# Own scores and row maxima as 128x128 tiles, the own weight spread through memory, value products in two runs a group

## The chip, the cores and the metric

One core of one Trainium2 chip runs the whole kernel. The metric is device time in microseconds, the median of a few executions. TensorE does the matrix products; VectorE, ScalarE and GpSimd do elementwise work; SyncE issues most transfers, and ScalarE issues some too.

## The reference

Eight batch rows of 512 tokens and 512 features pass two layers, each with a residual. The first is an attention whose softmax runs over 512 earlier keys and one key of the query's own:

```python
q = (query @ Wq + bq); k = (key @ Wk + bk); v = (value @ Wv + bv)       # 16 heads of 32
score_prev = einsum('bhqd,bhkd->bhqk', q, k[:, :, :l1]) * SCALE          # masked by seq_len1
score_self = (q * k[:, :, l1:]).sum(-1, keepdims=True) * SCALE           # the own score
weights = softmax(concatenate([score_prev, score_self], -1))
attn = einsum('bhqk,bhkd->bhqd', weights[..., :-1], v[:, :, :l1]) + weights[..., -1:] * v[:, :, l1:]
x = x + attn @ Wo + bo
```

The second is a feed-forward layer of 2048 hidden units, whose last 128 output columns use an expert's weights. Everything is float32; most products are made from a high and a low part.

## The kernel before, in words

The kernel has two stages. Stage one (to about 1090 us) makes the attention of all rows, stage two the output projection and the feed-forward layer. The change touches stage one alone.

The four 128-feature groups of a row (g = 0 to 3, four heads each) follow one another over the eight rows (batches): 32 groups. Each engine has its own written-out list of instructions. Every list walks a group in 16 steps (i = 0 to 15), one for each pair of a key tile t = i // 4 and a head j = i % 4. The first and the last batch are written out; the six between are a loop. While group G is attended, its successor G + 1 has its row maxima made, and G + 2 is projected.

TensorE's step i: the score tile (`ps_score`, L1173), which has two buffers and so waits until the exponential two tiles back is done (`p_made`); in steps 0 to 9 one or two tiles whose row maxima VectorE takes (`ps_max`, L1139 and L832); from step 4 on, four of the 48 products of the projections (L1109). After steps 1, 5, 9 and 13 four value products follow, one for each head (`value_burst`, L1186). They write strips of 32 partitions and run side by side. The denominators (L1195) come with the burst of step 5. In group 0 of a batch the values of the row are projected too (48 products).

The own score and the maximum go this way. Step 10: two products sum q*k over the heads into four rows (`own_scores`, L1147 and L1148); four small products turn the maxima into rows (`turn_max`, L1154). Step 11: ScalarE copies the own row (L593), VectorE takes the larger (`max_row`, L840), ScalarE and VectorE split its negative into `m_neg` (L601, L844). Step 12: ScalarE issues two transfers that put it into the operands of the next group's score tiles (`maxima`, L608). Step 13: three products make own score less maximum, spread over all 128 partitions (`own_less_max`, L1163 to L1165). Step 15: ScalarE takes its exponential into `den` (L615). Then GpSimd multiplies it into the own value, and VectorE adds the denominators, takes reciprocals (L882) and normalizes (L888).

GpSimd adds up each head's four probability tiles (`add_probabilities`, L507 and L510; 12 additions a group). It also makes the low parts of the next batch's inputs (`in_low`, L515): eight, spread over steps 10 to 13 of group 1 and 0 to 5 of group 2. VectorE's transposes of those inputs wait for them in turn. TensorE's projection at step 7 of group 2 waits for all eight:

```python
if n == 0:
    pe.wait_ge(in_lo_made, 2 * C * (b + 1))
```

## Time and profile before

| | us |
|---|---|
| median of 3 runs | 1920.85 (1918.96 to 1922.35) |
| the profiled execution | 1924.15, its span 1922.3 |
| TensorE matmuls busy | 1838.3 |
| VectorE busy | 965.4 |
| ScalarE busy | 752.9 |
| GpSimd busy (stage one alone) | 636.2 |

The span runs from the first to the last instruction; the rest of the profiled execution's time lies around it. Matmuls overlap in the trace: a product of 512 columns shows about 0.39 us, while its successor starts 0.23 us after it. So starts are to be read, not durations. A fp32 product stands as two records. ScalarE's issuing of transfers is not counted as busy.

### The profile page before, as it was taken

The numbers are of one execution on the slowest core, as the hardware profiler recorded it, in microseconds if no ns is written. First come the engines' busy times: TensorE is split into PE (matmuls) and PEld (weight loads), VectorE is DVE, ScalarE is ACT, GpSimd is POOL, SyncE is SP. The second block draws the span as 40 slices with busy tenths as digits, with TensorE's granted clock in tenths as the row PEclk, the third lists the DMA queues.
The fourth block names the chain that finished last, engine by engine and source line by source line (L and its number), as shares of the span: only waits on it lengthen the run. The fifth ranks groups of instructions, "written<-read, shape, count | busy, mean of one in ns | idle before, by whom it ended". The sixth has DMA issues, their size and how long they took to land.

```text
span 1922.3 us, 27293 instructions
## 1 busy us (share of the span) xinstructions
PE 1838.3 (96%) x8288; PEld 1300.6 (68%) x8288; DVE 965.4 (50%) x1373; ACT 752.9 (39%) x1290; POOL 636.2 (33%) x492
## 2 busy tenths in 40 slices
PE   6999999999999999999998799999999999999997
PEld 5656656556566565565564378888888888888886
DVE  4576576775775757757757552313232323232311
ACT  3354454444544544445434432323333332323222
POOL 3276484674764846747646400000000000000000
PEclk8999999999999999999999599999999999999999
DMA  6152342431623324316223431212131212122111
GB/s 142 35 116 57 70 83 71 78 82 39 121 59 73 78 67 82 77 40 120 64 53 88 126 94 39 50 38 50 33 55 33 50 37 38 47 33 51 27 22 22
DMA packets 337244, 122.17 MB, mean 64 GB/s; under 512 B 285642, under 2 KB 304074, under 8 KB 337170
## 3 DMA queue, kind: packets, MB, share of 16 engines
q1 hardware_dynamic: 336658, 120.83, 29.3%
q10 hardware_dynamic: 512, 0.53, 0.1%
q8 instruction: 26, 0.43, 0.1%
q14 instruction: 48, 0.39, 0.1%
HBM read 53.63 MB, written 16.79 MB: 37 GB/s over the span
## 4 chain that ended last, share of the span: by engine, by line
PE 85%; DVE 5%; issue 3%; POOL 3%; ACT 2%; SPq 2%; DMA 1%; ACTq 1%; DVEq 0%; POOLq 0%
PE ps_proj L1109 17%; PE ps_av L1061 6%; PE ps_av L1063 6%; PE ps_av L1062 6%; PE ps_av L1186 6%; PE ps_max L1139 6%; PE ps_score L1173 5%; PE ps_proj L1061 3%; PE ps_max L1063 3%; PE ps_score L1063 3%; PE ps_score L1062 3%; PE ps_max L1062 3%; PE ps_max L1061 3%; PE ps_score L1061 3%; PE ps_proj L1062 3%
## 5 line engine op out<-in xcount | busy, mean ns | idle before, releaser
L626 ACT ACTIVATE p_f<-ps_score 128x512 f32<-128x512 f32 x512 | 305.7, 599 | 499.3 <-PE ps_score L1173 415.7
L832 DVE TENSOR_REDUCE m_col<-ps_max 128x1 f32<-128x512 f32 x512 | 331.6, 684 | 237.8 <-PE ps_max L1139 237.4
L510 POOL TENSOR_TENSOR p_sum<-p_sum,p_f 128x512 f32<-128x512 f32 x256 | 344.1, 1357 | 113.8 <-ACT p_f L626 112.8
L994 DVE TENSOR_TENSOR h_lo<-h_f,h_hi 128x512 fp32r<-128x512 f32 x128 | 88.3, 690 | 480.0 <-ACT h_hi L723 479.9
L507 POOL TENSOR_TENSOR p_sum<-p_f 128x512 f32<-128x512 f32 x128 | 163.1, 1296 | 267.7 <-PE ps_av L1195 260.0
L1173 PE MATMUL ps_score<-stacks 99*128 99x512 f32 x512 | 216.8, 426 | 10.3 <-ACT p_f L626 9.6
L1139 PE MATMUL ps_max<-stacks 97*128 97x512 f32 x512 | 190.7, 428 | 31.6 <-DVE m_col L832 28.5
L1109 PE MATMUL ps_proj<-in_hi,w_hi 128*128 128x512 f32 x512 | 208.0, 406 | 10.9 <-POOL in_lo L515 7.6
L1109 PE MATMUL ps_proj<-in_lo,w_hi 128*128 128x512 f32 x512 | 206.4, 403 | 0.0
L1109 PE MATMUL ps_proj<-in_hi,w_lo 128*128 128x512 f32 x512 | 206.2, 403 | 0.0
L1061 PE MATMUL ps_av<-y_hi,w_hi 128*128 128x512 f32 x512 | 199.4, 390 | 1.5 <-DVE y_lo L990 1.5
L1063 PE MATMUL ps_av<-y_hi,w_lo 128*128 128x512 f32 x512 | 199.2, 389 | 0.0
L1062 PE MATMUL ps_av<-y_lo,w_hi 128*128 128x512 f32 x512 | 199.2, 389 | 0.0
L721 ACT ACTIVATE h_f<-ps_av,bias 128x512 f32<-128x512 f32 x128 | 88.2, 689 | 243.1 <-PE ps_av L1063 216.5
L723 ACT ACTIVATE h_hi<-ps_av,bias 128x512 fp32r<-128x512 f32 x128 | 88.2, 689 | 208.2 <-PE ps_max L1063 208.2
L1139 PEld LDWEIGHTS ps_max<-stacks 97*128 97x128 f32 x512 | 97.5, 190 | 104.6 <-DVE m_col L832 85.6
L1186 PE MATMUL ps_av<-p_f,v_st 128*32 128x512 f32 x1024 | 144.3, 627 | 5.0 <-ACT p_f L626 4.9
L1173 PEld LDWEIGHTS ps_score<-stacks 99*128 99x128 f32 x512 | 97.5, 191 | 74.9 <-ACT p_f L626 39.7
L1109 PEld LDWEIGHTS ps_proj<-in_hi,w_hi 128*128 128x128 f32 x512 | 97.9, 191 | 55.1 <-issue 32.8
L1109 PEld LDWEIGHTS ps_proj<-in_hi,w_lo 128*128 128x128 f32 x512 | 97.6, 191 | 45.4 <-issue 25.2
L1109 PEld LDWEIGHTS ps_proj<-in_lo,w_hi 128*128 128x128 f32 x512 | 97.9, 191 | 41.5 <-issue 25.1
L882 DVE RECIPROCAL den<-den 128x128 f32<-128x128 f32 x128 | 112.2, 918 | 0.7
(129 smaller groups left out, 2863.3 us busy)
## 6 DMA issues: line engine op xcount, KB each, us to landing
stacks<-parts SPq DMA_DIRECT2D x384, 128.0 KB
raw<-in_x_dram SPq DMA_DIRECT2D x128, 64.0 KB, 2.1
raw<-in_fside_BxSxS_dram SPq DMA_DIRECT2D x128, 64.0 KB, 2.2
attn_scratch<-num SPq DMA_DIRECT2D x32, 256.0 KB, 2.3
x_raw<-in_x_dram SPq DMA_DIRECT2D x128, 64.0 KB, 2.1
a_raw<-attn_scratch SPq DMA_DIRECT2D x32, 256.0 KB, 3.2
we_raw<-in_L_cond_We_dram SPq DMA_DIRECT2D x32, 256.0 KB, 2.8
out_dram<-z_t SPq DMA_DIRECT2D x128, 64.0 KB, 1.9
```

Of the source, the lines that this page charges most:

```text
L507: pool.tensor_tensor(p_sum[:, j], p_f[:, j], now, ALU.add).then_inc(sum_made, 1)
L510: pool.tensor_tensor(p_sum[:, j], p_sum[:, j], now, ALU.add).then_inc(sum_made, 1)
L626: act.activation(p_f[:, i % FLIGHT], ps_score[i % 2][:, :], ACT.Exp, scale=SCALE).then_inc(p_made, 1)
L832: dve.tensor_reduce(m_col[:, n % C, n // C:n // C + 1], ps_max[n % 2][:, :], AX.X, ALU.max).then_inc(max_made, 1)
L882: dve.reciprocal(den[:, r, at], den[:, r, at]).then_inc(rden_made, 1)
L1061: pe.matmul(ps, left[0], right[0], start=first, stop=False)
L1062: pe.matmul(ps, left[0], right[1], start=False, stop=False)
L1063: return pe.matmul(ps, left[1], right[0], start=False, stop=last)
L1109: mm = pe.matmul(ps, left, right, start=(m == 0), stop=(m == 3 * C - 1))
L1139: pe.matmul(ps_max[n % 2][:, :], q_st[0:KM, r, j, P * t:P * (t + 1)], k_st[0:KM, r, j, :], start=True, stop=True).then_inc(max_mm, 1)
L1173: pe.matmul(ps_score[i % 2][:, :], k_st[0:KS, r, j, P * t:P * (t + 1)], q_st[0:KS, r, j, :], start=True, stop=True).then_inc(score_mm, 1)
L1186: pe.matmul(ps_num[at, :], v_st[:, t, P * g + DH * j:P * g + DH * (j + 1)], p_f[:, i % FLIGHT], start=(t == 0), stop=(t == C - 1)).then_in ...
```

## The change

- The sum over heads and the turned maxima are each four fp32 products of 128 columns that write the four strips of a 128x128 tile. Partition 32t + j holds head j for the queries of tile t. The split of q*k into high and low parts is gone.
- The copy, the maximum and its two parts work on 128x128 tiles. VectorE takes own score less maximum (`own_less_max`), ScalarE its exponential, in place in `own_s`.
- Eight transfers instead of two put the maxima into the score operands.
- The own weight is stored to memory by ScalarE and read back, spread over 32 partitions for each head, by four transfers of SyncE (`own_weights`). The three products at step 13 are gone.
- The value products of key tiles 2 and 3 come at step 2 of the next group, those of tiles 0 and 1 at step 10, with the denominators, own scores and turned maxima behind them. There are 16 probability buffers instead of 8.
- GpSimd's additions run from step 11 to step 6 of the next group; VectorE's denominator, reciprocals and normalization stand at steps 12 to 15.

```diff
     TILES = HG * C
-    FLIGHT = 2 * HG
+    FLIGHT = 4 * HG
...
     attn_dram = nc.dram_tensor("attn_scratch", (B, C, P, S), F32, kind="Internal").ap()
+    own_dram = nc.dram_tensor("own_scratch", (2, C, DH, P), F32, kind="Internal").ap()
...
+        own_s = sb1("own_s", [P, P])
+        m_s = sb1("m_s", [P, P])
+        m_neg = sb1("m_neg", [P, 2, P], F32R)
+        m_col = sb1("m_col", [P, C, DH])
+        sum_heads = sb1("sum_heads", [P, DH])
...
+            def own_weights(b, c):
+
+                G, r = C * b + c, c % 2
+                sp.wait_ge(ow_stored, DMA * (G + 1))
+                wait(sp, attn_made, G - 1)
+                for j in range(HG):
+                    sp.dma_start(den[DH * j:DH * (j + 1), r].rearrange("d (t q) -> d t q", q=P),
+                                 own_dram[r, :, j].partition_broadcast(DH)).then_inc(ow_landed[r], DMA)
...
+                    if not (last and g == C - 1):
+                        own_weights(*after(b, g, 1))
...
-                pool.wait_ge(ow_made, G + 1)
+                pool.wait_ge(ow_landed[c % 2], HG * DMA * (2 * b + c // 2 + 1))
...
                                 in_low(b + 1, j)
-                        if i == 3:
+                        if i == 8:
                             own_value(b, g)
-                        if i >= HG:
-                            add_probabilities(b, g, i // HG, i % HG)
+                        n = (i + 5) % TILES
+                        if i >= 11:
+                            add_probabilities(b, g, 1 + n // HG, n % HG)
+                        elif n < SUMS and not (first and g == 0):
+                            add_probabilities(*after(b, g, -1), 1 + n // HG, n % HG)
             batches(pool, batch)
+            for n in range(5, SUMS):
+                add_probabilities(B - 1, C - 1, 1 + n // HG, n % HG)
...
-                    act.dma_start(f(q_st[KM + n:KM + n + 1, r]),
-                                  f(m_neg[QUAD * n:QUAD * n + HG])).then_inc(m_landed[r], DMA)
+                    for t in range(C):
+                        act.dma_start(f(q_st[KM + n:KM + n + 1, r, :, P * t:P * (t + 1)]),
+                                      f(m_neg[DH * t:DH * t + HG, n])).then_inc(m_landed[r], DMA)
...
             def own_weight(b, c):
                 G = C * b + c
-                act.wait_ge(ow_mm, G + 1)
-                wait(act, attn_made, G - 1)
-                act.activation(den[:, c % 2], ps_max[1][:, :], ACT.Exp, scale=SCALE).then_inc(ow_made, 1)
+                act.wait_ge(own_less_made, G + 1)
+                act.activation(own_s[:, :], own_s[:, :], ACT.Exp, scale=SCALE).then_inc(ow_made, 1)
+                pb, pc = after(b, c, -2)
+                wait(act, ow_landed[c % 2], HG * DMA * (2 * pb + pc // 2 + 1))
+                act.wait_ge(ow_made, G + 1)
+                act.dma_start(own_dram[c % 2].rearrange("t k q -> (t k) q"), own_s[:, :]).then_inc(ow_stored, DMA)
...
-                if t < 2:
-                    wait(act, sum_made, sums_of(C * b + g - 1, t + 2, j))
-                else:
-                    act.wait_ge(sum_made, sums_of(C * b + g, 1, j))
+                wait(act, sum_made, sums_of(C * b + g - 1, max(t, 1), j))
...
+            def own_less_max(b, c):
+                dve.wait_ge(m_s_made, C * b + c + 1)
+                dve.tensor_tensor(own_s[:, :], own_s[:, :], m_s[:, :], ALU.subtract).then_inc(own_less_made, 1)
...
-                        if i == 5 and bound:
-                            qk_low(*nxt)
-                        if i == 3 and started:
+                        if i == 4 and started:
                             numerator(*after(b, g, -1))
-                        if i == 7 and started:
+                        if i == 12 and started:
                             denominator(*after(b, g, -1))
                         if not last:
                             for j in turn_at.get((g, i), ()):
@@ -944,17 +937,18 @@
                         if i == 8 and project:
                             k_low(*nxt2)
                         if i == 11 and bound:
-                            max_row(*nxt)
+                            own_max(*nxt)
                         if i == 11 and project:
                             q_low(*nxt2)
                         if i == 11 and bound:
                             m_low(*nxt)
-                        if i in (10, 13) and started:
-                            for n in range(2) if i == 10 else range(2, 4):
+                            own_less_max(*nxt)
+                        if i in (13, 14) and started:
+                            for n in range(2) if i == 13 else range(2, 4):
                                 one_over_den(*after(b, g, -1), n)
                         if i == 13 and project:
                             qk(*nxt2)
-                        if i == 14 and started:
+                        if i == 15 and started:
                             normalize(*after(b, g, -1))
...
             def own_scores(b, c):
                 G = C * b + c
-                pe.wait_ge(qk_lo_made, G + 1)
+                pe.wait_ge(qk_f_made, G + 1)
                 pe.wait_ge(max_made, TILES * (G + 1))
-                pe.matmul(ps_max[1][0:HG, :], sum_heads[:, :], qk_hi[:, :], start=True, stop=False)
-                pe.matmul(ps_max[1][0:HG, :], sum_heads[:, :], qk_lo[:, :], start=False, stop=True).then_inc(own_mm, 1)
+                for t in range(C):
+                    mm = pe.matmul(ps_max[1][DH * t:DH * (t + 1), 0:P], sum_heads[:, :], qk_f[:, P * t:P * (t + 1)],
+                                   start=True, stop=True)
+                mm.then_inc(own_mm, 1)
             def turn_max(b, c):
                 pe.wait_ge(max_made, TILES * (C * b + c + 1))
                 for t in range(C):
-                    mm = pe.matmul(ps_max[0][0:HG, P * t:P * (t + 1)], m_col[:, t, :], f(ident[:, :]), start=True, stop=True)
+                    mm = pe.matmul(ps_max[0][DH * t:DH * (t + 1), 0:P], m_col[:, t, :], f(ident[:, :]), start=True, stop=True)
                 mm.then_inc(turn_mm, 1)
-
-            def own_less_max(b, c):
-
-                G = C * b + c
-                pe.wait_ge(own_made, G + 1)
-                pe.wait_ge(m_lo_made, G + 1)
-                ps = ps_max[1][:, :]
-                pe.matmul(ps, sum_spread[:, :], qk_hi[:, :], start=True, stop=False)
-                pe.matmul(ps, sum_spread[:, :], qk_lo[:, :], start=False, stop=False)
-                pe.matmul(ps, spread[:, :], m_neg[:, :], start=False, stop=True).then_inc(ow_mm, 1)
...
-                        if i == 1 and not (first and g == 0):
-                            value_burst(*after(b, g, -1), C - 1)
-                        if i > 1 and i % HG == 1:
-                            value_burst(b, g, i // HG - 1)
-                        if i == HG + 1 and not (first and g == 0):
-                            denominators(*after(b, g, -1))
                         if g == 0 and not first and 1 <= i < 1 + C:
                             values(b, i - 1)
                         if more and i >= 4:
                             project(*nxt2, order[(i - 4) // 3], (i - 4) % 3)
+                        if i == 2 and not (first and g == 0):
+                            for t in (2, 3):
+                                value_burst(*after(b, g, -1), t)
+                        if i == 10:
+                            for t in (0, 1):
+                                value_burst(b, g, t)
+                            if not (first and g == 0):
+                                denominators(*after(b, g, -1))
                         if bound and i == 10:
                             own_scores(*nxt)
                             turn_max(*nxt)
-                        if bound and i == 13:
-                            own_less_max(*nxt)
             batches(pe, batch)
+            value_burst(B - 1, C - 1, C - 2)
```

On TensorE, before, from the score tile of step 10 to that of step 14 (the projections' products also stand there, before and now, and are left out):

```order
L1173 MATMUL ps_score<-stacks 128x512
...
L1147 MATMUL ps_max<-qk_hi,sum_heads 4x512
L1148 MATMUL ps_max<-qk_lo,sum_heads 4x512
L1154 MATMUL ps_max<-ident,m_col 4x128 x4
L1173 MATMUL ps_score<-stacks 128x512
L1173 MATMUL ps_score<-stacks 128x512
L1173 MATMUL ps_score<-stacks 128x512
L1186 MATMUL ps_av<-p_f,v_st 32x512 x4
L1163 MATMUL ps_max<-qk_hi,sum_spread 128x512
L1164 MATMUL ps_max<-qk_lo,sum_spread 128x512
L1165 MATMUL ps_max<-m_neg,spread 128x512
L1173 MATMUL ps_score<-stacks 128x512
```

Now, from step 10 to step 14:

```order
L1159 MATMUL ps_score<-stacks 128x512
L1172 MATMUL ps_av<-p_f,v_st 32x512 x8
L1181 MATMUL ps_av<-p_sum,ones 32x512 x4
L1142 MATMUL ps_max<-qk_f,sum_heads 32x128 x4
L1150 MATMUL ps_max<-ident,m_col 32x128 x4
L1159 MATMUL ps_score<-stacks 128x512
L1159 MATMUL ps_score<-stacks 128x512
L1159 MATMUL ps_score<-stacks 128x512
L1159 MATMUL ps_score<-stacks 128x512
```

All strip products of the group's second half now stand in one run at step 10, and steps 11 to 15 hold only score tiles and projections.

On ScalarE, steps 11 to 15 before:

```order
L593 COPY m_row<-ps_max 4x512
L626 ACTIVATE p_f<-ps_score 128x512
L601 ACTIVATE m_neg<-m_row 4x512
L626 ACTIVATE p_f<-ps_score 128x512
L608 DMA stacks<-m_neg 1x4x512 x2
L626 ACTIVATE p_f<-ps_score 128x512 x2
L615 ACTIVATE den<-ps_max 128x512
```

and now:

```order
L594 COPY own_s<-ps_max 128x128
L627 ACTIVATE p_f<-ps_score 128x512
L601 ACTIVATE m_neg<-m_s 128x128
L627 ACTIVATE p_f<-ps_score 128x512
L609 DMA stacks<-m_neg 1x4x128 x8
L627 ACTIVATE p_f<-ps_score 128x512 x2
L615 ACTIVATE own_s<-own_s 128x128
L619 DMA own_scratch<-own_s 128x128
```

Nine issues stand where two stood, eight of them between the exponentials of steps 12 and 13.

On GpSimd, from the remainder of step 12 of group 1 to the last one, at step 5 of group 2, before (additions L507 and L510, remainders L515, own value L498):

```order
L515 TENSOR_TENSOR in_lo<-turned,in_hi 128x512
L510 TENSOR_TENSOR p_sum<-p_sum,p_f 128x512
L515 TENSOR_TENSOR in_lo<-turned,in_hi 128x512
L510 TENSOR_TENSOR p_sum<-p_sum,p_f 128x512 x3
L515 TENSOR_TENSOR in_lo<-turned,in_hi 128x512 x2
L498 TENSOR_TENSOR v<-v,den 128x512
L515 TENSOR_TENSOR in_lo<-turned,in_hi 128x512
L507 TENSOR_TENSOR p_sum<-p_f 128x512
L515 TENSOR_TENSOR in_lo<-turned,in_hi 128x512
```

and now:

```order
L517 TENSOR_TENSOR in_lo<-turned,in_hi 128x512
L509 TENSOR_TENSOR p_sum<-p_f 128x512
L517 TENSOR_TENSOR in_lo<-turned,in_hi 128x512
L509 TENSOR_TENSOR p_sum<-p_f 128x512 x2
L512 TENSOR_TENSOR p_sum<-p_sum,p_f 128x512
L517 TENSOR_TENSOR in_lo<-turned,in_hi 128x512
L512 TENSOR_TENSOR p_sum<-p_sum,p_f 128x512 x2
L517 TENSOR_TENSOR in_lo<-turned,in_hi 128x512
L512 TENSOR_TENSOR p_sum<-p_sum,p_f 128x512 x2
L517 TENSOR_TENSOR in_lo<-turned,in_hi 128x512
L512 TENSOR_TENSOR p_sum<-p_sum,p_f 128x512
L517 TENSOR_TENSOR in_lo<-turned,in_hi 128x512
```

Among the six remainders stood five additions and the own value; now nine additions stand there.

## Rows read from the trace of the kernel before

**Rows 1.** The page's first part: busy us, share of the span, instructions, by engine.

```profile
PE 1838.3 (96%) x8288; PEld 1300.6 (68%) x8288; DVE 965.4 (50%) x1373; ACT 752.9 (39%) x1290; POOL 636.2 (33%) x492
```

**Rows 2.** TensorE's waits from 100 to 1090 us: total, times, longest.

```profile
PE ps_max L1139 <- DVE m_col L832: 27.6, 66, 0.9
```

**Rows 3.** TensorE's timeline in one group: start us, duration us, instruction.

```profile
604.77 0.40 PE L1147 MATMUL ps_max<-qk_hi,sum_heads 128*4 128x512 f32 x1
...
605.33 1.04 PE L1154 MATMUL ps_max<-ident,m_col 128*4 128x128 f32 x8
...
606.30 0.50 PE L1173 MATMUL ps_score<-stacks 99*128 99x512 f32 x1
...
606.63 0.40 PE L1109 MATMUL ps_proj<-in_lo,w_hi 128*128 128x512 f32 x1
...
608.72 0.39 PE L1173 MATMUL ps_score<-stacks 99*128 99x512 f32 x1
...
610.37 0.39 PE L1109 MATMUL ps_proj<-in_lo,w_hi 128*128 128x512 f32 x1
...
611.07 0.39 PE L1163 MATMUL ps_max<-qk_hi,sum_spread 128*128 128x512 f32 x1
...
612.40 0.40 PE L1109 MATMUL ps_proj<-in_lo,w_hi 128*128 128x512 f32 x1
...
622.35 1.07 PE L1186 MATMUL ps_av<-p_f,v_st 128*32 128x512 f32 x8
...
623.23 1.04 PE L1195 MATMUL ps_av<-p_sum,ones 128*32 128x512 f32 x8
```

**Rows 4.** ScalarE's timeline about its two transfers; ACTq is its queue.

```profile
540.58 0.60 ACT L626 ACTIVATE p_f<-ps_score 128x512 f32<-128x512 f32 x1
542.13 1.22 ACTq L608 DMA_DIRECT2D stacks<-m_neg  x2
543.54 0.60 ACT L626 ACTIVATE p_f<-ps_score 128x512 f32<-128x512 f32 x1 [2.37 <-POOL p_sum L510]
```

**Rows 5.** Three lines that issue transfers: ns of one issue, min/median/max.

```profile
L608 ACTq DMA_DIRECT2D stacks<-m_neg x64: 580/587/1182, 69.4 to 1052.2; - x64
...
L323 SPq DMA_DIRECT2D stacks<-parts x384: 552/598/2155, 37.8 to 1028.0; - x192
...
L319 SPq DMA_DIRECT2D stacks<-mask_scratch x64: 229/309/712, 37.5 to 960.0; - x64
```

**Rows 6.** VectorE's timeline at the end of the same group.

```profile
540.64 1.46 DVE L844 SCALAR_TENSOR_TENSOR m_neg<-m_row,m_neg 4x512 fp32r<-4x512 f32 x1 [0.30 <-ACT m_neg L601]
542.12 1.76 DVE L882 RECIPROCAL den<-den 128x128 f32<-128x128 f32 x2
...
544.38 1.75 DVE L888 TENSOR_TENSOR num<-num,den 128x512 f32<-128x512 f32 x1
```

**Rows 7.** VectorE's groups by line over the span: busy, mean ns.

```profile
L860 DVE TENSOR_TENSOR den<-ps_av,den 128x512 f32<-128x512 f32 x32 | 21.7, 679 | 0.0
```

**Rows 8.** TensorE's timeline from group 1 to group 2 of a batch.

```profile
507.72 0.50 PE L1173 MATMUL ps_score<-stacks 99*128 99x512 f32 x1
...
530.58 0.40 PE L1173 MATMUL ps_score<-stacks 99*128 99x512 f32 x1
...
538.88 0.50 PE L1173 MATMUL ps_score<-stacks 99*128 99x512 f32 x1
```

**Rows 9.** GpSimd's additions, a group of the page: busy, mean ns, idle before.

```profile
L510 POOL TENSOR_TENSOR p_sum<-p_sum,p_f 128x512 f32<-128x512 f32 x256 | 344.1, 1357 | 113.8 <-ACT p_f L626 112.8
```

**Rows 10.** GpSimd's timeline: the last of the eight remainders for the next batch.

```profile
529.30 1.29 POOL L515 TENSOR_TENSOR in_lo<-turned,in_hi 128x512 fp32r<-128x512 f32 x1
```

**Rows 11.** TensorE in 10 us: window, length, busy, granted clock, DMA share, GB/s.

```profile
140.00:150.00 10.00, 10.00 (x45) 0.84 0.00 0
```

**Rows 12.** The last maxima: their two transfers and the score tile behind them.

```profile
1051.55 1.20 ACTq L608 DMA_DIRECT2D stacks<-m_neg  x2
...
1055.34 0.80 PE L1173 MATMUL ps_score<-stacks 99*128 99x512 f32 x1 [0.58 <-DMA stacks<-m_neg]
```

More of the change, by code:

```diff
@@ L191, in cond_resid_program @@
         turn_mm = sem("turn_mm")
-        m_row_made, m_hi_made, m_lo_made = sem("m_row_made"), sem("m_hi_made"), sem("m_lo_made")
+        m_s_made, m_hi_made, m_lo_made = sem("m_s_made"), sem("m_hi_made"), sem("m_lo_made")
         m_landed = [sem(f"m_landed{r}") for r in range(2)]
-        ow_mm, ow_made = sem("ow_mm"), sem("ow_made")
+        own_less_made, ow_made = sem("own_less_made"), sem("ow_made")
+        ow_stored = sem("ow_stored")
+        ow_landed = [sem(f"ow_landed{r}") for r in range(2)]
         score_mm = sem("score_mm")
```

81 lines of the change are left out of this document (25 added, 56 removed).

## The prediction

> **What bounds the kernel now.** I read four views in this order. The page's first part says that TensorE is the engine to follow: it is busy nearly all the span, the others half of it at most [rows 1]. The waits say that in stage one it stands still for little, above all for VectorE's maxima, 27.6 us in 66 waits [rows 2]. So a cut in TensorE's own work is time gained, as long as nothing new makes it wait. The timelines then give the price of each piece of its work as a distance between starts, and what the other engines do meanwhile. The lines on transfers give what an issue costs the engine that issues it.
>
> I measure from the start of the score tile of step 11 (call it 0), in a group with projections. Before, two such tiles lie 31.16 us apart where group 2 of a batch lies between [rows 8].
>
> **TensorE's own work: what goes.** A product of 512 columns takes a slot of 0.23 us: the three from 610.37 to 611.07 take 0.70. The sum over heads and the turned maxima take 606.63 - 604.77 less one slot = 1.63 us. The three products at step 13 take 612.40 - 611.07 less one slot = 1.10. A burst of value products alone takes 610.37 - 608.72 less two slots = 1.19; behind another burst it takes 623.23 - 622.35 = 0.88. So starting and leaving a run of strip products costs 0.31 [rows 3]. Before: five bursts (denominators included) in four runs, 5 x 0.88 + 4 x 0.31 = 5.64, and 1.63 + 1.10: 8.37 us a group. Now: 5 x 0.88 + 2 x 0.31 = 5.02 and X for own scores and turned maxima, all inside the second run.
>
> X is not in this trace. From below: the turned maxima now take 0.97 us for eight records in a row (605.33 to 606.30), of which a third of the 0.31 is leaving; four strips at once would take a quarter of 0.86, 0.22 for each of the two, 0.44 together. From above: strips of 128 columns that don't overlap, 2 x 0.86 = 1.7. The bursts are the nearest rows: eight records of 1.07 us length in 0.88, so strips overlap; I take 0.6. TensorE's work falls by 8.37 - 5.62 = 2.75 us a group (1.65 to 2.9).
>
> **ScalarE: what is added.** An issue on its queue takes 0.587 us in the median, 0.580 at least. SyncE's transfers between the same memories, sixteen times the bytes, take 0.598. Only a transfer of one row that starts in DRAM takes 0.31 [rows 5]. The engine does nothing else meanwhile: the two issues run from 542.13 to 543.35, and the next exponential, whose score had long been there, starts at 543.54 [rows 4]. The new eight have the same four rows on either side, only shorter, so I take 0.61 each as in that pair, 4.9 us; the ends are 0.3 and 0.64. The store of the own weight adds one more, 0.4.
>
> Walk through it. Score tiles follow every 5 x 0.23 = 1.16 us, the first after 1.26: steps 12 to 15 would start at 1.26, 2.42, 3.58 and 4.74, the next group at 5.90. The exponential of step 12 starts 1.7 after the zero (538.88 to 540.58) [rows 4, 8]. VectorE's low part of the maxima ended at 3.2 before (540.64 + 1.46) [rows 6]; on 128 columns and with GpSimd adding beside it I put it at 2.5 (2.1 to 2.9). Eight issues end at 7.4, the exponential of step 13 runs from 7.6 to 8.2. Score tile 15 waits for it: 8.25 instead of 4.74, a stall of 3.5. The next group's first score tile could start at 9.4, but needs the maxima landed. In the last group a tile that waited for them started 2.6 us after the issues' end (1051.55 + 1.20 to 1055.34) [rows 12], which gives 10.0. Then own weight, store and the exponential of step 15 end at 10.2, and the second score tile is due at 10.7 instead of 6.6. The stall is 3.9 us, since the maxima behind it waited some 0.2 anyway (27.6 us in 66 waits) [rows 2]. Net for such a group: 3.9 - 2.75 = +1.15.
>
> The Trainium skill says otherwise. "DMA: Bandwidth & Descriptors", section "Issuing engines are not separate DMA queues", holds the sequencer's time to initiate a transfer to be usually small beside the transfer itself. By it the eight issues would cost nothing and the gain of 2.75 would arrive; the pair of issues in this trace held ScalarE for 1.22 us, so I go by the rows.
>
> **VectorE at the group's end.** Denominator (0.68), four reciprocals (2 x 1.76) and normalization (up to 1.75) now all stand behind the maxima's parts, with q*k (about 0.65) [rows 6, 7]. That is 6.6 us behind about 3.3, so it ends at 7.9 to 10.1. Beside the stall on ScalarE it costs nothing. If ScalarE were quick it would be late itself: the next maxima would wait 0.7 to 2.9 us.
>
> **GpSimd from group 1 to 2.** The last remainder ended at 530.59, and the score tile of step 7 started at 530.58, its projection right behind it: 22.9 us after zero [rows 8, 10]. So it is already tight. Now the remainder of step 13 waits for ScalarE behind the eight issues and ends at about 10.2. Eight additions and four remainders must follow before the projection may start. At 1.32 us each (1.29 for the remainder [rows 10], 1.36 in the mean for the additions [rows 9]) that is 26.0. TensorE needs 8.5 us more to the next zero (21 slots, 4.9, and the second run, 3.6), with the wait's latency 34.7 instead of 31.16: +3.6 (+1 if the issues are cheap, +5 with each addition slowed). In this stretch none of the 2.75 arrives.
>
> **The clock.** A stall of 3.5 us in one piece is new. Before, the clock fell on a few occasions after thinly filled stretches: in the ten microseconds from 140 the mean is 0.84 of full speed, 2.4 GHz with some time at 1.2 GHz, at most 1.6 us of work lost [rows 11]. One such dip a group costs 0 to 1.6; much of it falls on the start of a group, where VectorE sets the pace, so I take 0.5. The Trainium skill, "TensorE: Matmul & The Clock Gate", section "Why this matters for your kernels", asks for no idle gaps between bursts, since the clock falls in them; by it every group would dip, the upper end.
>
> **What is hidden.** The way of the own weight through memory has from step 15 to step 8 of the next group, over 12 us; it needs about 7, five issues of 0.31 to 0.44 and two landings of at most 2.6 us. If it came late, GpSimd's own product would wait, and nobody reads that before the next group. Sixteen buffers free the exponentials from the late bursts. In the last group the additions start at step 10 instead of 5 and end about 4 us later.
>
> **Sum.** Of 30 groups with projections behind step 11, seven lead from group 1 to 2: 23 x 1.15 = 26; 7 x 3.6 = 25; clock 30 x 0.5 = 15; tail 4. Together +70, against the profiled execution's 1924 us: 1994. That execution lies 3 us over the median of the runs, so I predict 1990.
>
> **The rivals.**
> Cheap issues: 0.31 each, as for the row from DRAM. They end at 5.0, score tile 15 waits 1.1 us, and VectorE's late normalization adds about 1.5. The stall of 2.6 eats the 2.75: 23 x -0.15, 7 x 1.5, tail 4: +11, 1932. For it: shorter rows. Against: the issue's time did not follow the size between 8 and 128 KB.
> The work arrives: ScalarE's issues don't hold up the exponentials and VectorE keeps pace. 23 x -2.75, 7 x -0.5: -65, 1856. Against: [rows 4].
> X is high, strips of 128 columns one after another: +1.1 a group on the forecast, 2025.
> Stalls without a dip of the clock: 1975, inside my range.
> That the change doesn't do what it says is out: its order drops two of four runs of value products and five wide products a group; only X is open.
> The point where the sign turns is the issue's price: with 0.61 the stall is 3.9, and it falls under 2.75 where an issue costs below 0.46 (3.9 less eight times the difference), if VectorE keeps pace.
>
> **Chances.** The forecast with its variants (with or without dips, X up to high) 0.78: 1960 to 2040. Cheap issues 0.12: 1905 to 1950. The work arrives 0.10: 1845 to 1880. The range of 8 in 10 is 1915 to 2035. The forecast is slower by far; cheap issues give half slower, a quarter each of the rest. A measurement here can tell about 0.2% from no change. So slower 0.84, within 0.2% 0.03, faster 0.13.
>
> **What would show it.** Right: in the profile after, TensorE waits for the exponential at its score tile about 3 us once a group, thirty times, right behind eight issues of 0.6 us on ScalarE's queue; its strip products and own scores take about 5.6 us a group in two runs; remainders hold a projection back in group 2; the clock's tenths fall in stage one. Wrong: issues of 0.3 us, score tiles at even distances through steps 12 to 15, or bursts of own scores that take over a microsecond. Stage two should keep its length.

## The result, and the profile after

The changed kernel takes 2046.6 us in the median of four runs (2041.2 to 2047.2), the kernel before 1921.0 beside it: ratio 1.065, interval 1.063 to 1.067. I had predicted 1990 with a range up to 2035. The sign was right and the size was not: +126 us instead of +70. The profiled execution has a span of 2039.4 us, 117 us over the one before.

The page's first part and its slices, against [rows 1]: matmul records take as long as before (1841.8 us for 1838.3) and so a smaller share of a longer span (90% for 96%), and the granted clock now stands at eight tenths of full speed through most of stage one.

```profile
PE 1841.8 (90%) x8384; PEld 1325.0 (65%) x8384; DVE 959.1 (47%) x1367; ACT 713.0 (35%) x1258; POOL 632.7 (31%) x489
PEclk8988888889879889888888769999999999999999
```

The same line of the page before:

```profile
PEclk8999999999999999999999599999999999999999
```

TensorE's waits (us in total, times, longest), against [rows 2]: VectorE's maxima cost less than before, and the exponential has taken over.

```profile
PE ps_score L1159 <- ACT p_f L627: 144.5, 45, 11.7
PE ps_max L1133 <- DVE m_col L823: 11.8, 38, 0.5
PE ps_proj L1103 <- POOL in_lo L517: 7.7, 5, 3.6
```

ScalarE's timeline in one group, whose score tile of step 11 (zero, as in the prediction) starts at 620.66. It answers to [rows 4]:

```profile
622.52 0.60 ACT L627 ACTIVATE p_f<-ps_score 128x512 f32<-128x512 f32 x1 [0.37 <-PE ps_score L1159]
623.53 4.99 ACTq L609 DMA_DIRECT2D stacks<-m_neg  x8
628.78 1.08 ACT L627 ACTIVATE p_f<-ps_score 128x512 f32<-128x512 f32 x2 [5.66 <-POOL p_sum L512]
630.15 0.33 ACTq L619 DMA_DIRECT2D own_scratch<-own_s  x1
```

Eight issues hold the engine for 4.99 us; the exponential of step 13 starts 8.1 us after zero (GpSimd, named as its releaser, had long been done). TensorE's timeline of the same stretch, against [rows 3]:

```profile
620.11 0.40 PE L1142 MATMUL ps_max<-qk_f,sum_heads 128*32 128x128 f32 x8
620.33 0.40 PE L1150 MATMUL ps_max<-ident,m_col 128*32 128x128 f32 x8
620.66 0.50 PE L1159 MATMUL ps_score<-stacks 99*128 99x512 f32 x1
...
624.27 0.40 PE L1159 MATMUL ps_score<-stacks 99*128 99x512 f32 x1
...
629.43 0.80 PE L1159 MATMUL ps_score<-stacks 99*128 99x512 f32 x1 [3.84 <-ACT p_f L627]
630.03 0.63 PE L1103 MATMUL ps_proj<-in_hi,w_lo 128*128 128x512 f32 x1
630.45 0.63 PE L1103 MATMUL ps_proj<-in_hi,w_hi 128*128 128x512 f32 x1
```

Own scores and turned maxima take 0.22 us each (620.11 to 620.33 to 620.66, the last with the step to the next product). Score tile 15 starts 8.8 us after zero, having waited 3.84. Behind it the products stand 0.43 us apart (two of the lines above) instead of 0.23. The windows of the group before it (zero at 587.20) say why; their columns are the stretch, its length, each engine's busy time, the granted clock, the memory share and GB/s:

```profile
587.00:592.00 5.00, 5.00 (x32) 3.70 (x20) 4.47 (x6) 1.66 (x4) 5.00 (x4) 1.00 0.25 56
592.00:597.00 5.00, 1.05 (x3) 0.82 (x3) 4.66 (x6) 1.28 (x3) 5.00 (x5) 0.81 0.72 161
597.00:602.00 5.00, 5.00 (x12) 3.03 (x11) 2.08 (x4) 2.64 (x5) 5.00 (x5) 0.50 0.63 145
602.00:607.00 5.00, 4.96 (x21) 1.36 (x21) 1.76 (x3) 0.79 (x2) 2.03 (x2) 0.67 0.23 76
607.00:612.00 5.00, 4.73 (x20) 3.79 (x21) 4.54 (x8) 1.83 (x4) 0.00 (x0) 1.00 0.00 0
```

TensorE stands still from 592 to 597 but for 1.05 us, and then works at 1.2 GHz instead of 2.4. With 0.81, 0.50 and 0.67 in windows of five microseconds, 10.2 us lie at half clock. It is as much behind every wait of groups 0, 1 and 2 but the very first and one in the last batch. Behind the wait of group 3, which the timeline above shows, it is 3.4 us, spread over two windows:

```profile
627.00:632.00 5.00, 2.57 (x6) 2.09 (x7) 3.13 (x5) 1.88 (x4) 5.00 (x5) 0.72 0.72 162
632.00:637.00 5.00, 4.69 (x19) 3.48 (x19) 1.97 (x3) 1.58 (x3) 4.27 (x4) 0.94 0.61 164
```

Note that PE shows "5.00 busy" in the window from 597, the worst of them: a busy share says nothing of the speed.

The table is the measure used from here on: the median distance in us between the score tiles of step 11, by the groups between which it lies (8, 8, 7 and 7 distances; the very last one is left out), read from the timelines. "Lost clock" is the share of 200 to 1000 us lost to the half clock, one less the granted clock of that window.

| kernel | 0 to 1 | 1 to 2 | 2 to 3 | 3 to 0 (values) | median us | lost clock |
|---|---|---|---|---|---|---|
| before | 28.9 | 31.2 | 28.8 | 38.6 | 1921.0 | 0.00 |
| changed | 33.6 | 34.9 | 33.4 | 41.4 | 2046.6 | 0.12 |
| 1: two transfers | 30.1 | 34.0 | 30.3 | 38.7 | 1965.4 | 0.05 |
| 2: eight, new layout | 32.0 | 35.0 | 33.7 | 42.7 | 2048.8 | 0.10 |
| 3: products in the stall | 30.2 | 34.9 | 30.1 | 40.0 | 2005.4 | 0.02 |
| 4: before, six more issues | 32.1 | 34.6 | 33.4 | 41.9 | 2051.3 | 0.06 |
| 7: before, three more | 29.8 | 33.2 | 29.1 | 38.8 | 1944.0 | 0.01 |
| 6: before, six to DRAM | 30.8 | 33.9 | 30.1 | 39.7 | 1982.9 | 0.03 |
| 5: two transfers, eased | 27.2 | 32.1 | 30.0 | 37.4 | 1913.8 | 0.03 |
| 8: strips by head | 28.1 | 33.0 | 28.2 | 38.2 | 1916.8 | 0.01 |
| 9: and transposes later | 28.1 | 32.9 | 28.1 | 38.2 | 1916.6 | 0.02 |
| 10: eight, eased | 31.7 | 34.8 | 33.9 | 42.8 | 2041.2 | 0.11 |
| 11: two small moves on 5 | 27.3 | 32.1 | 30.8 | 37.3 | 1917.9 | 0.04 |

### The profile page after: what moved, and what is told of

Read it like the earlier page. It is cut to its first block, busy times and chain, and to the rows that moved or that the text cites. A ratio compares the mean times of both kernels' runs of the same rounds, so it can differ in the third digit from the quotient of the medians.

```text
span 2039.4 us, 27891 instructions
## 1 busy us (share of the span) xinstructions
PE 1841.8 (90%) x8384; PEld 1325.0 (65%) x8384; DVE 959.1 (47%) x1367; ACT 713.0 (35%) x1258; POOL 632.7 (31%) x489
## 4 chain that ended last, share of the span: by engine, by line
PE 73%; ACTq 8%; DVE 6%; POOL 4%; issue 4%; ACT 2%; SPq 1%; DMA 1%; POOLq 0%; DVEq 0%
PE ps_proj L1103 12%; ACTq L609 7%; PE ps_av L1172 6%; PE ps_max L1133 6%; PE ps_av L1055 6%; PE ps_av L1057 6%; PE ps_av L1056 6%; PE ps_score L1159 5%; PE ps_max L1055 3%; PE ps_score L1055 3%; PE ps_max L1056 3%; PE ps_score L1056 3%; PE ps_max L1057 3%; PE ps_score L1057 3%; PE ps_proj L1055 3%
## 5 line engine op out<-in xcount | busy, mean ns | idle before, releaser
L1159 PE MATMUL ps_score<-stacks 99*128 99x512 f32 x512 | 242.7, 475 | 145.8 <-ACT p_f L627 144.5
L512 POOL TENSOR_TENSOR p_sum<-p_sum,p_f 128x512 f32<-128x512 f32 x256 | 331.9, 1326 | 7.4 <-ACT p_f L627 7.3
L509 POOL TENSOR_TENSOR p_sum<-p_f 128x512 f32<-128x512 f32 x128 | 177.7, 1414 | 341.4 <-PE ps_av L1181 341.4
L1159 PEld LDWEIGHTS ps_score<-stacks 99*128 99x128 f32 x512 | 110.7, 217 | 229.3 <-ACT p_f L627 164.3
L1133 PE MATMUL ps_max<-stacks 97*128 97x512 f32 x512 | 211.0, 476 | 12.4 <-DVE m_col L823 11.8
L1103 PE MATMUL ps_proj<-in_hi,w_lo 128*128 128x512 f32 x512 | 217.6, 425 | 0.0
L1133 PEld LDWEIGHTS ps_max<-stacks 97*128 97x128 f32 x512 | 112.4, 220 | 91.1 <-DVE m_col L823 68.2
L1172 PE MATMUL ps_av<-p_f,v_st 128*32 128x512 f32 x1024 | 159.3, 748 | 1.6 <-ACT p_f L627 1.6
L517 POOL TENSOR_TENSOR in_lo<-turned,in_hi 128x512 fp32r<-128x512 f32 x64 | 82.4, 1288 | 147.1 <-ACT in_hi L560 147.1
L1103 PEld LDWEIGHTS ps_proj<-in_hi,w_lo 128*128 128x128 f32 x512 | 106.4, 208 | 22.1
```

What stands on the lines that cost most here:

```text
L509: pool.tensor_tensor(p_sum[:, j], p_f[:, j], now, ALU.add).then_inc(sum_made, 1)
L512: pool.tensor_tensor(p_sum[:, j], p_sum[:, j], now, ALU.add).then_inc(sum_made, 1)
L1103: mm = pe.matmul(ps, left, right, start=(m == 0), stop=(m == 3 * C - 1))
L1133: pe.matmul(ps_max[n % 2][:, :], q_st[0:KM, r, j, P * t:P * (t + 1)], k_st[0:KM, r, j, :], start=True, stop=True).then_inc(max_mm, 1)
L1159: pe.matmul(ps_score[i % 2][:, :], k_st[0:KS, r, j, P * t:P * (t + 1)], q_st[0:KS, r, j, :], start=True, stop=True).then_inc(score_mm, 1)
L1172: pe.matmul(ps_num[at, :], v_st[:, t, P * g + DH * j:P * g + DH * (j + 1)], p_f[:, i % FLIGHT], start=(t == 0), stop=(t == C - 1)).then_in ...
```

## The experiments

My theory after the result: the eight issues stall TensorE as forecast, and its clock falls behind the stall, which I had priced far too low. The rivals: the clock falls because value products now stand in dense runs or because of the memory traffic; or the new orders of VectorE and GpSimd cost the time by themselves.

**1. Two transfers instead of eight.**

```diff
-                    for t in range(C):
-                        act.dma_start(f(q_st[KM + n:KM + n + 1, r, :, P * t:P * (t + 1)]),
-                                      f(m_neg[DH * t:DH * t + HG, n])).then_inc(m_landed[r], DMA)
+                    act.dma_start(f(q_st[KM + n:KM + n + 1, r]),
+                                  f(m_neg[0:P:DH // HG, n])).then_inc(m_landed[r], DMA)
```

> The changed kernel with the maxima put in by two transfers of 16 x 128 instead of eight of 4 x 128. To make that one pattern on each side, a head's row stands at every eighth partition of its strip, and the stacks are laid out by query tile first, for which SyncE's stacks take four transfers a head instead of three; all other work is as in the changed kernel. Theory 1 (eight issues on ScalarE stall TensorE, and the stall lets its clock fall): the issues take 1.2 us instead of 4.8, the wait of the score tile for the exponential (144.5 us in 45 waits) goes to under 20 us, the stretch at half clock in each group goes, and what is left is TensorE's saving less what VectorE and GpSimd hold back: a group at 27 to 28.5 us between the score tiles of step 11 instead of 33.5, in all 1890 us (1870 to 1915). Theory 2 (the clock falls because all value products now stand in two dense runs): the half clock stays, 2000 or more. Theory 3 (VectorE, with reciprocals and normalization at the group's end, takes the place of the stall): near the kernel before, 1915 to 1945, with PE waiting for m_col more than 60 us.

1965.4 us, ratio 1.024 (1.020 to 1.029). TensorE's wait for the exponential fell from 144.5 to 30.7 us (44 times). 81 of the 126 us are gone, but the time is above the ranges of theories 1 and 3 and below that of theory 2. The sign of theory 3 is there: its waits for VectorE's maxima, 11.8 us in the changed kernel, are now over 60. The line of the waits, then one of them in TensorE's timeline:

```profile
PE ps_max L1135 <- DVE m_col L825: 88.9, 69, 4.2
```

```profile
499.23 0.50 PE L1135 MATMUL ps_max<-stacks 97*128 97x512 f32 x1 [2.50 <-DVE m_col L825]
```

VectorE's list in front of that maximum:

```profile
493.80 1.76 DVE L879 RECIPROCAL den<-den 128x128 f32<-128x128 f32 x2
495.48 0.65 DVE L816 SCALAR_TENSOR_TENSOR qk_f<-ps_proj,bias,q_f 128x512 f32<-128x512 f32 x1
496.05 1.75 DVE L879 RECIPROCAL den<-den 128x128 f32<-128x128 f32 x2
497.83 0.74 DVE L885 TENSOR_TENSOR num<-num,den 128x512 f32<-128x512 f32 x1
498.50 2.63 DVE L825 TENSOR_REDUCE m_col<-ps_max 128x1 f32<-128x512 f32 x4
```

And the windows around it:

```profile
495.00:500.00 5.00, 2.50 (x10) 1.40 (x9) 4.97 (x8) 2.12 (x4) 5.00 (x5) 1.00 0.71 159
500.00:505.00 5.00, 4.89 (x22) 1.57 (x22) 1.86 (x4) 0.71 (x2) 4.61 (x4) 0.66 0.53 121
```

Zero is 489.03. VectorE's list ends 9.5 us after it (the prediction: 7.9 to 10.1), the maximum is 2.5 us late (0.7 to 2.9), and a half clock follows this wait too. In group 1 of each batch the same wait is 4.1 us. So the eight issues hid a second cost, VectorE's list, which shows once they are gone. In the first group, where VectorE has no denominator yet, the distance is 27.5 against 28.9 before.

**2. Its control.** The eight transfers, with the stacks laid out as in the first.

```diff
-        stacks = sb1("stacks", [P, 2, HG, 2, S], F32R)
+        stacks = sb1("stacks", [P, 2, 2, C, HG, P], F32R)
```

> The control of the first: the changed kernel, eight transfers of 4 x 128 kept, only the stacks laid out by query tile first and SyncE's four stack transfers a head. Every theory of the eight issues expects the changed kernel's time, 2047 us within 8; if the layout or SyncE's extra issues matter, it shows here.

2048.8 us, ratio 1.065 (1.063 to 1.067): for the time the layout does not matter, the issues do. (The single distances differ: from 0 to 1 several dips of the clock are shorter here, and with values longer.)

**3. The stall kept, TensorE fed in it.**

```diff
+                        if bound and i == TILES - 1:
+                            for n in range(18):
+                                pe.matmul(ps_max[1][:, P:S], k_st[0:KS, g % 2, HG - 1, 0:P],
+                                          q_st[0:KS, g % 2, HG - 1, P:S], start=True, stop=True)
                         score_tile(b, g, i)
```

> The changed kernel with 18 products of 384 columns that nobody reads, put ahead of the score tile of step 15 in every group that prepares another: about 3.2 us at full clock, in the place where TensorE stands still for 3.8 us behind the eight issues. The issues and the wait stay. If the stall causes the fall of the clock (theory 1), the half clock goes, and a group falls from 33.5 to about 29.7 us as in the one group that had no dip: 30 x 3.8 less, 1935 us (1925 to 1965). If the clock falls for another reason (dense runs of strip products, or memory traffic), it stays at 2040 or more, since the products only fill the wait; a partial dip would be between.

2005.4 us, ratio 1.041 (1.036 to 1.046). TensorE's timeline and the windows of a group:

```profile
652.62 3.29 PE L1213 MATMUL ps_max<-stacks 99*128 99x384 f32 x18
656.88 0.50 PE L1159 MATMUL ps_score<-stacks 99*128 99x512 f32 x1 [0.97 <-ACT p_f L627]
```

```profile
652.00:657.00 5.00, 4.03 (x23) 3.58 (x22) 4.93 (x7) 0.77 (x2) 5.00 (x5) 1.00 0.82 183
657.00:662.00 5.00, 4.62 (x21) 2.45 (x25) 3.60 (x6) 3.21 (x7) 5.00 (x4) 1.00 0.48 111
662.00:667.00 5.00, 4.69 (x26) 2.78 (x19) 3.07 (x6) 1.73 (x3) 2.78 (x3) 1.00 0.77 168
```

Issues, merged runs and memory traffic are all there, and the exponential comes as late; only TensorE's idleness is not, and the half clock is gone: 33.6 becomes 30.2. So idleness is the cause, and dense runs and traffic are not. My 1935 was wrong in three ways. Between groups 1 and 2 nothing came back (34.9 both times): without the half clock TensorE waits there for GpSimd's remainders, 0.4 to 1.0 us in each batch. With values 1.4 us came back and not 3.8, as the dip there is short. And in the profiled execution (2009.9 us) four groups were still long, 36.1 to 47.6 us, 27 us together. They have one cause: VectorE's normalization, which stands ahead of a maximum, took 6.90 us in each of the four and about 0.75 in most others. TensorE then waited 4.9 to 5.4 us, and its clock fell behind each of these waits. One of the four:

```profile
167.02 6.90 DVE L883 TENSOR_TENSOR num<-num,den 128x512 f32<-128x512 f32 x1
```

Why it took so long is open; no other run here shows it.

**4, 7 and 6. The kernel before, with spare issues alone.** All its orders are kept. Six or three transfers of four rows of 128 follow the two of the maxima on ScalarE's queue, into SBUF or (6) into DRAM.

```diff
+                for n in range(6):
+                    act.dma_start(spare[:, n], f(m_neg[0:HG, 0:P])).then_inc(spare_landed, DMA)
```

> The kernel before with six more transfers of 4 x 128 floats from the maxima's tile to a spare one, issued on ScalarE's queue right behind the two that put the maxima in; no engine waits for them but at the stage's end. The exponential of step 13 would end at about 8.9 us after the score tile of step 11 instead of 5.3; score tile 15 stands at 7.0 there, so TensorE stalls 1.9 us. Theory 1: 31 x 1.9 = +59 us from the stall alone, 1980, and with a fall of the clock in each group of the size seen in the changed kernel, up to 31 x 5.7 = 2097; I expect the clock to fall in part, 2010. If an issue of these costs 0.31, the stall is 0.1 us and the time stays at 1921 to 1930. If the new orders of the other engines are what costs the time, it stays there too.

> As the fourth experiment, with three more transfers to SBUF instead of six: 1.8 us less of issues, a stall of about 1.2 us instead of 3.1. If the clock's loss is in proportion to the stall, the 128 us of the six become about 50 (1971); if a stall of this length leaves the clock alone, 31 x 1.2 = 37: 1958; if any stall behind the issues brings the full dip of 3.4 us a group, 2060.

> As the fourth experiment (2051 us), but the six more transfers of 4 x 128 floats go to a spare place in DRAM instead of one in SBUF. Their issues took 0.58 us each in the median there, 4.3 us together, and TensorE stalled 3.1 us. The store of the own weight to DRAM in the changed kernel took 0.33. If the kind of memory sets the issue's time, six take 2.0 us, the stall falls to about 0.8 us, and the time to 1950 (1935 to 1975), with few dips of the clock. If the small transfers on this queue cost 0.58 whatever the memory, 2051 stays.

2051.3 us (ratio 1.067, 1.064 to 1.069), 1944.0 (1.011, 1.009 to 1.012) and 1982.9 (1.032, 1.029 to 1.035). Six issues alone, in the old kernel, cost as much as the change. That the sums agree is chance: the change also takes work off TensorE, and its wait is longer (3.6 to 4.8 us a group against 1.7 to 3.2). My forecasts were 2010 for the fourth, 1958 or 1971 for the seventh (2060 with the full dip) and 1950 for the sixth, and all three missed. In the fourth I had put the wait at 1.9 us; in the seventh at 1.2, and it was nothing in two groups of each batch, 0.7 and 1.6 in the others; in the sixth I had put an issue at 0.33 us, and it took 0.42. The spare issues' durations (ns: least, median, most) in the seventh, then the sixth:

```profile
L614 ACTq DMA_DIRECT2D spare<-m_neg x96: 580/583/1031, 71.0 to 1073.3; - x96
```

```profile
L614 ACTq DMA_DIRECT2D spare<-m_neg x192: 306/422/887, 70.8 to 1110.2; - x192
```

ScalarE's timeline of the fourth in one group, and the windows of the next; TensorE's wait is 3.09 us in the first, which is a group 1, and 1.85 in the next, behind which the clock falls:

```profile
561.98 1.22 ACTq L611 DMA_DIRECT2D stacks<-m_neg  x2
563.22 4.28 ACTq L614 DMA_DIRECT2D spare<-m_neg  x6
567.69 0.60 ACT L631 ACTIVATE p_f<-ps_score 128x512 f32<-128x512 f32 x1 [6.31 <-issue]
```

```profile
600.00:604.00 4.00, 2.38 (x8) 1.95 (x9) 0.00 (x0) 2.33 (x5) 2.28 (x2) 0.85 0.71 160
604.00:608.00 4.00, 4.00 (x13) 1.16 (x13) 1.98 (x3) 1.92 (x4) 2.72 (x3) 0.50 0.52 142
```

The series shows that the price of a wait rises with its length. Between groups 2 and 3 a wait of 0.95 us (experiment 6) costs 1.2 us; one of 1.85 us (experiment 4) costs 3.3 to 5.4. Three issues cost 21 us, six cost 128: twice the issues, six times the time. Much of that is the wait itself, which begins only where the issues outlast ScalarE's slack: TensorE waited 29.3, 55.6 and 84.3 us for exponentials at its score tiles in experiments 7, 6 and 4, against 9.6 before. These 20, 46 and 75 us more cost 21, 60 and 128 us: 1.1, 1.3 and 1.7 us for each. So a cost in proportion to the stall is out.

**5. Two transfers, and what stood in TensorE's way moved.**

```diff
-                        if i == 10:
+                        if i == 8 and not (first and g == 0):
+                            denominators(*after(b, g, -1))
...
-                        if i >= 11:
+                        if i >= 9:
                             add_probabilities(...)
...
-                        if i == 12 and started:
+                        if i == 9 and started:
                             denominator(*after(b, g, -1))
+                        if i == 10 and started:
+                            for n in range(2):
+                                one_over_den(*after(b, g, -1), n)
```

> The two-transfer kernel of the first experiment (1965 us), with what stood there in the way of TensorE moved: the denominators' products at step 8 instead of 10, GpSimd's additions from step 9 of their group instead of 11, VectorE's denominator at step 9 and two of the four reciprocals at step 10, the others at 12 and the normalization at 14. There VectorE's list ended 9.4 us after the score tile of step 11 and TensorE waited 2.5 us in one piece for a maximum, after which its clock fell; now 2.4 us of that list lie in VectorE's idle time ahead of that tile (4.4 us). Theory 1 (TensorE's own saving of 2.75 us a group was real and was hidden by waits, and the clock falls behind a long wait): no half clock in ordinary groups, 26.7 us a group with the 0.31 of the extra run; from group 1 to 2 GpSimd starts its additions 3 us earlier, 31 instead of 34; with values 36; a batch 120 instead of 127.5: 1875 us (1855 to 1905). If the clock falls because of the merged runs or the traffic of memory, or the saving isn't real: 1920 or more.

1913.8 us, ratio 0.9952 (0.9938 to 0.9967): the version that beats both, by 0.5% and 6.5%. Between groups 0 and 1 the distance is 27.2 (28.9 before): there the saving arrives. Not so elsewhere. From 2 to 3 the stacks are late, since they now take four issues of SyncE for each head, and the window behind them stands at 0.66:

```profile
544.39 0.71 PE L1138 MATMUL ps_max<-stacks 97*128 97x512 f32 x2 [0.60 <-DMA stacks<-parts]
547.81 0.71 PE L1138 MATMUL ps_max<-stacks 97*128 97x512 f32 x1 [1.07 <-DMA stacks<-parts]
```

```profile
547.00:552.00 5.00, 4.19 (x18) 1.10 (x19) 1.17 (x2) 0.17 (x1) 0.76 (x1) 0.66 0.47 102
```

My 1875 counted on 31 us from 1 to 2 and 120 for a batch; it was 32.1 and 127.

**8 and 9. Strips by head,** which gives the stacks their three issues back; in the ninth also three transposes later.

```diff
-                for t in range(C):
-                    mm = pe.matmul(ps_max[1][DH * t:DH * (t + 1), 0:P], sum_heads[:, :], qk_f[:, P * t:P * (t + 1)],
-                                   start=True, stop=True)
+                for t in range(C):
+                    for j in range(HG):
+                        at = slice(DH * j, DH * (j + 1))
+                        mm = pe.matmul(ps_max[1][at, 0:P], sum_heads[at, t], qk_f[at, P * t:P * (t + 1)],
+                                       start=(t == 0), stop=(t == C - 1))
```

> The fifth experiment (1914 us) with the strips of the 128x128 tile by head instead of by query tile, a query tile's row at every eighth partition: then the maxima lie as the stacks have them, two transfers put them in, and SyncE's stacks take three transfers a head again instead of four (twelve issues of 0.62 us a group instead of sixteen). The own scores become sixteen products of 32x32 on 128 columns instead of four of 128x32. In the fifth experiment TensorE waited 18.2 us for the stacks in 25 waits, and a group from 2 to 3 took 30.0 us against 27.3 from 0 to 1. If the fourth issue a head is what makes the stacks late: those waits gone, 27.5 us from 2 to 3, and with 1 us less from 1 to 2: 1885 us (1875 to 1905). If sixteen small products cost a microsecond more than the four, the gain is lost: 1914.

> The eighth with three of VectorE's transposes of the next batch a step or two later (from steps 14 and 15 of group 1 and step 3 of group 2 to 15, 0 and 4), since in the fifth experiment three of them stood ahead of the first maximum there and TensorE waited 1.6 us for it. GpSimd was busy from 510 to 528 without a gap, so it shouldn't need them sooner: 0.7 to 1.4 us less in each of seven groups, 5 to 10 us under the eighth. If GpSimd runs dry instead, the projection waits for its remainder and the time is the same or more.

1916.8 us (0.997, 0.996 to 0.998) and 1916.6 (0.997, 0.996 to 0.998). The waits for stacks are gone and 2 to 3 fell to 28.2, as it should if the fourth issue made them late. But every group pays for the small products:

```profile
602.99 0.40 PE L1153 MATMUL ps_max<-ident,m_col 128*32 128x128 f32 x8
603.32 1.08 PE L1144 MATMUL ps_max<-qk_f,sum_heads 32*32 32x128 f32 x32
604.32 0.50 PE L1162 MATMUL ps_score<-stacks 99*128 99x512 f32 x1
```

They take 1.00 us with the step to the next product. Turned maxima and own scores together take 1.33 us against 0.55 in the changed kernel, 0.8 us more: the second expectation of the eighth. The later transposes changed nothing.

**10. The moves alone, with eight transfers.** The edits of the fifth on the changed kernel.

> The changed kernel with its eight transfers kept, and the moves of the fifth experiment alone (denominators' products at step 8, additions from step 9, VectorE's denominator and reciprocals earlier): the fourth corner beside the changed kernel (2047 us), two transfers (1965) and both (1914). If the eight issues and the clock behind them are the main cause, the moves can't show while ScalarE is held up: the stall of 3.9 us and the half clock stay in every group; only from group 1 to 2 GpSimd's earlier start gives 2 to 3 us: 2030 us (2020 to 2045). If the orders of VectorE and GpSimd were the main cause, the 51 us that the moves gave with two transfers come here too: 1995.

2041.2 us, ratio 1.062 (1.061 to 1.064), inside the range. The moves give 52 us with two transfers and 5 with eight; the transfers give 81 without the moves. GpSimd's earlier start did not help from 1 to 2 (34.8), as I had expected it to: the waits for its remainders in group 2 are gone, but in the changed kernel they were only 0.12 to 0.37 us each; stall and half clock take nearly the same time there. In six of eight places from 0 to 1 the same wait of 4.2 us was followed by a shorter dip (a window at 0.68, the next at 0.97) and 31.7 us, 3.4 us at half clock instead of 10.2. Experiment 2 has such short dips as well, without the moves. What sets a dip's length stays open.

**11. Two small moves on the fifth:** the low part of q ahead of the maximum on VectorE, the own weight behind the exponential of step 15.

> The fifth experiment (1914 us) with two small moves: VectorE makes the low part of q ahead of its maximum at step 11 (it idles 1.1 us there), so that SyncE's stacks can start up to a microsecond sooner, against which TensorE waited 18.2 us in 25 waits; and ScalarE's own weight and its store come behind the exponential of step 15 instead of ahead of it, against waits of the score tile of 0.3 us. If TensorE's waits there are bound by these two, 0.8 us less in each of 23 groups: 1898 us (1890 to 1908). If the maximum comes later by it (the exponentials of the maxima's sign and the issues behind it all shift), the gain is eaten: 1914, or a few microseconds more.

1917.9 us, ratio 0.998 (0.996 to 0.999): nothing gained. The stacks did not come sooner for it: TensorE waited 26.1 us for them instead of 18.2.

## Why the prediction was right and wrong

**The failed step: the clock.** I took 0.5 us for each of 30 groups, 15 in all, "since much of it falls on the start of a group". Experiment 3 gives the size by difference: 3.4 us from 0 to 1 and from 2 to 3, 1.4 with values, none from 1 to 2 (33.6 less 30.2, and so on). For 30 distances the profiled changed kernel has 110.5 us more than the profiled kernel before; at the medians of experiment 3 it would have 8 x 1.2 + 8 x 3.7 + 7 x 1.2 + 7 x 1.5 = 58. So the clock took 52 us, 37 more than I had put in. Experiment 4 shows a loss of that size in the old order: 128 us for 75 of added waits. I took the price from [rows 11], a stretch thin by many small waits with a clock of 0.84. The trace of before had stalls in one piece too, and I overlooked them: in the last group TensorE stood still for 2.47 us up to 1051.66 and went on with further waits, and its clock was at half from 1051 to 1072. [rows 12] come from that very stretch, and their score tile shows 0.80 us; its windows:

```profile
1045.00:1050.00 5.00, 3.74 (x21) 1.32 (x21) 5.00 (x5) 1.17 (x2) 3.96 (x3) 1.00 0.28 94
1050.00:1055.00 5.00, 3.09 (x5) 1.36 (x5) 3.07 (x6) 3.83 (x8) 2.51 (x2) 0.62 0.33 108
1055.00:1060.00 5.00, 1.92 (x6) 0.78 (x10) 3.88 (x5) 2.70 (x6) 2.59 (x3) 0.50 0.41 129
```

They don't give the price of a dip in a full group. But they show a dip far longer than that of [rows 11], whose clock of 0.84 over ten microseconds is 3.2 us at half. In the changed kernel 10.2 us at half clock lose 5.1 us of work, of which 3.4 come through; the 3.4 us of group 3 lose 1.7, of which 1.4 do. My upper bound of 1.6 was no bound. The Trainium skill, "TensorE: Matmul & The Clock Gate", section "Why this matters for your kernels", was the rule I quoted and priced as the upper end; the trace agrees with it in every group but the first, which kept its clock, with a stall of 3.57 us against 3.69 to 4.77 in the 29 others.

**The issues: right.** 0.594 us in the median against 0.61 taken (4.99 for the eight, 4.9 taken), score tile 15's stall 3.84 against 3.5 (3.9 was the delay of the tiles behind it), the exponential of step 13 at 8.1 for 7.6. The rival of cheap issues is out: they cost 0.31 to 0.42 only where DRAM is an end (experiment 6), and 2 KB cost what 128 KB cost [rows 5]. "DMA: Bandwidth & Descriptors", section "Issuing engines are not separate DMA queues", in the Trainium skill, calls the initiation usually small beside the transfer. It was not for these: 0.59 us an issue, where the two transfers of the maxima in experiment 5 took 2.1 us from issue to landing. And experiment 4 lost 128 us to the issues of data that nobody reads.

**The net of an ordinary group: right.** +1.15 forecast; +0.79 in the first group, whose clock stayed up, and +1.2 in experiment 3. **The saving of 2.75: right but unseen.** X, taken at 0.6, is 0.44, my lower bound. The fifth experiment gained 1.7 from 0 to 1 with 0.31 for its extra run and 0.5 of waiting: 2.5. **Group 1 to 2: right, in part by luck.** +3.6 forecast, +3.7 measured. The last remainder ends 26.6 us after zero (26.0), and the projection starts right behind it, here after a zero at 552.29:

```profile
577.64 1.29 POOL L517 TENSOR_TENSOR in_lo<-turned,in_hi 128x512 fp32r<-128x512 f32 x1
```

But TensorE waited for it only 0.15 us. Its stall of 4.58 us and the half clock, which I had not put in here, brought it to that point almost as late by themselves; experiment 3 takes the clock's part away and has the same 34.9, experiment 10 takes GpSimd's away and has 34.8.

**VectorE behind quick issues: right** by experiment 1 in ordinary groups (2.5 us), and too low in group 1 (4.1). **The rest.** Without the clock the forecast was 55 us (26 + 25 + 4); measured are 58 for the distances and 7 for the ends, 65. With the 52 of the clock that makes the 117 us between the two profiled executions; the medians lie 126 apart, since the changed kernel was profiled in its quickest run. The range failed with the clock's bound alone: "stalls without a dip" was written as a rival below my forecast, and no rival had a dip in every group at its full price. Two smaller things: the 0.2 us that I took off the stall doesn't follow from 27.6 us in 66 waits, which is 0.4 each. And the own weight came later to GpSimd than I thought, which waited 32.6 us in 24 waits for it from 100 to 1200 us; GpSimd then stands idle for TensorE anyway (341.4 us in 24 waits).

## What to carry to other kernels

An issue on an engine's own queue is an instruction of that engine: count the issues, not the bytes, and ask what the engine should have done meanwhile. A stall in one piece is dearer than its length: a wait of one microsecond cost 1.2 us here, waits of 1.7 to 3.2 us in experiment 4 cost 2 to 7, because TensorE came back at 1.2 GHz. The price of a stall is to be looked for in the stretches of the old trace where such a stall stood, even if they are few and at the ends. When such a wait can't be removed, see whether other work can stand in it. A saving on the busiest engine shows only when the next in line (here VectorE's list, the stacks, GpSimd's remainders) keep pace.

## What the runs showed of the hardware

- Eighteen products that nobody reads, in a stall, made the kernel 41 us faster (2046.6 to 2005.4).
- An issue on ScalarE's queue took 0.58 us from SBUF to SBUF for 2 KB, and 0.31 at least, 0.42 in the median, to DRAM.
- Four fp32 products of 128 columns into four strips took 0.22 us; sixteen of 32 rows each, four to a strip, took 1.00 with the step to the next product.
- Stalls of about 4 us in the changed kernel were followed by no dip once, by 3.4 us at half clock in group 3 of each batch, and by 10.2 us in the other groups but one. In experiments 2 and 10 some other stalls of that length were followed by 3.4 us too. Why is open.
- A two-input operation of VectorE on 128x512, 0.75 us in most groups of experiment 3, took 6.90 us four times. Why is open.
